# Reordering batch 0 between its ternary layer and its first softmax, in a float32 network of two attention and two feed-forward layers

## What is computed

```python
x = x + _L0_xattn_ref(_layernorm(x), fside_BxS2xS2_0, ctx_1024)     # int8-like quantised linear, silu, quantised linear
x = x + _L0_ffn_ref(_layernorm(x), w1, w2, w3)                      # ternary weights: sigmoid(x1) * x2, down
x = x + _L1_xattn_ref(_layernorm(x), ctx_1024, mask, Wq, Wk, Wv, Wo)  # 16 heads, softmax over 256 context rows
x = x + _L1_ffn_ref(_layernorm(x), router, sh_gate, sh_up, sh_down, r_gate, r_up, r_down)  # gated, plus routed part
```

## Time and profile before

| | us |
|---|---|
| median of 3 runs | 388.93 |
| lowest and highest | 388.9 and 389.31 |
| the profiled execution | 389.01 |
| its span, first to last instruction | 387.3 |
| TensorE busy in it | 377.5 (97%) |
| VectorE, ScalarE, GpSimd busy | 299.0, 233.2, 162.3 |

### The profile page before, as it was taken

How to read it: one execution, slowest core, us unless ns; L and a number is a source line. 1 busy time by engine, 2 the same in 40 slices (tenths; PEclk the granted TensorE clock), 3 DMA queues, 4 the chain that set the end, 5 groups by cost and what they waited for, 6 DMA issues and landing times.

```text
span 387.3 us, 8390 instructions
## 1 busy us (share of the span) xinstructions
PE 377.5 (97%) x2966; PEld 357.2 (92%) x2966; DVE 299.0 (77%) x982; ACT 233.2 (60%) x616; POOL 162.3 (42%) x260
## 2 busy tenths in 40 slices
PE   8899999999999999999999999999999999999996
PEld 7798789999899999999999999999999999999896
DVE  4798889889967889787767989787768876665644
ACT  1798787867544466766554466766554676664332
POOL 2113876874633344344443345246343333332232
PEclk9999999999999999999999999999999999999999
DMA  7999310000000200000000200000000000000000
GB/s 246 324 341 391 115 32 2 2 2 0 3 2 0 85 1 3 0 3 3 2 27 2 59 1 2 0 3 3 1 29 2 0 3 0 3 0 2 24 8 27
DMA packets 15193, 16.93 MB, mean 44 GB/s; under 512 B 1584, under 2 KB 14128, under 8 KB 15152
## 3 DMA queue, kind: packets, MB, share of 16 engines
q1 hardware_dynamic: 15152, 16.40, 13.0%
HBM read 15.34 MB, written 1.05 MB: 42 GB/s over the span
## 4 chain that ended last, share of the span: by engine, by line
PE 80%; DVE 11%; ACT 4%; POOL 2%; issue 2%; DVEq 0%; POOLq 0%
PE bank_qa L409 12%; PE bank_o L663 7%; PE bank_s L608 7%; PE bank_pt L628 7%; PE bank_u L644 7%; PE bank_s L409 5%; PE bank_o L667 4%; PE bank_s L616 3%; PE bank_u L648 3%; PE bank_s L526 3%; PE bank_pt L409 3%; PE bank_u L748 3%; PE bank_pt L556 2%; PE bank_pt L526 1%; PE bank_x L418 1%
## 5 line engine op out<-in xcount | busy, mean ns | idle before, releaser
L1318 POOL TENSOR_SCALAR prob<-prob,row_inv,valid_b 128x256 f32<-128x256 f32 x128 | 70.3, 559 | 84.9 <-DVE row_inv L1688 84.9
L1014 ACT ACTIVATE prob<-prob,row_min 128x256 f32<-128x256 f32 x128 | 64.2, 502 | 39.6 <-DVE row_min L1680 39.5
L1693 DVE TENSOR_TENSOR pt_lo<-bank_pt,pt_hi 128x512 fp32r<-128x512 f32 x64 | 43.9, 685 | 14.9 <-ACT pt_hi L967 14.9
L1680 DVE CUSTOM_DVE_ANT_0 prob<-bank_s,masked 128x256 f32<-128x256 f32 x128 | 48.5, 417 | 0.9 <-ACT masked L996 0.6
L1329 POOL TENSOR_TENSOR act_lo<-act_raw,act_hi 128x256 fp32r<-128x256 f32 x32 | 24.2, 755 | 44.3 <-ACT act_hi L1081 44.2
L967 ACT ACTIVATE pt_hi<-bank_pt 128x512 fp32r<-128x512 f32 x64 | 37.6, 587 | 4.0 <-PE bank_pt L628 3.8
L628 PE MATMUL bank_pt<-ident,prob 128*128 128x128 f32 x256 | 39.2, 274 | 0.4 <-POOL prob L1318 0.3
L608 PE MATMUL bank_s<-cxT_hi,qa_hi 128*128 128x256 f32 x128 | 37.9, 319 | 0.0
L409 PE MATMUL bank_qa<-xt_hi,a_hi 128*128 128x256 f32 x126 | 35.6, 283 | 0.0
L409 PE MATMUL bank_qa<-xt_lo,a_hi 128*128 128x256 f32 x126 | 35.5, 282 | 0.0
L409 PE MATMUL bank_qa<-xt_hi,a_lo 128*128 128x256 f32 x126 | 35.5, 282 | 0.0
(11 more groups left out here) (325 smaller groups left out, 1196.3 us busy)
## 6 DMA issues: line engine op xcount, KB each, us to landing
wq_raw<-in_wqT SPq DMA_DIRECT2D x4, 512.0 KB, 7.9
wo_raw<-in_wo SPq DMA_DIRECT2D x4, 512.0 KB, 8.4
w_raw<-in_w12T SPq DMA_DIRECT2D x2, 704.0 KB, 7.7
gate_raw<-in_gateT SPq DMA_DIRECT2D x2, 576.0 KB, 7.6
up_raw<-in_upT SPq DMA_DIRECT2D x2, 576.0 KB, 9.4
down_raw<-in_downT SPq DMA_DIRECT2D x2, 576.0 KB, 11.2
x<-in_x SPq DMA_DIRECT2D x4, 256.0 KB, 6.1
guT<-in_guT SPq DMA_DIRECT2D x4, 256.0 KB, 3.5
```

Of the source, the lines that this page charges most:

```text
L1014: act.activation(row, row, ACT.Exp, scale=-1.0, bias=row_min[:, h % 2, t:t + 1], accum_out=row_sum[:, h % 2, t:t + 1]).then_inc(S["s_exp"], 1)
L1318: pool.tensor_scalar(row, row, row_inv[:, h % 2, t:t + 1], valid_b[:, 0:1], ALU.mult, ALU.mult).then_inc(S["s_norm"], 1)
L1680: dve.tensor_tensor_reduce(out=prob[:, h % 2, t, :], in0=src[:, t * T:(t + 1) * T], in1=masked[:, :], scale=1.0, scalar=3.0e38, op0=ALU.ad ...
L1693: dve.tensor_tensor(pt_lo[:, :, cols], bank["pt"][:, :].rearrange("p (s t) -> p s t", s=2), f32(pt_hi[:, :, cols]), ALU.subtract).then_inc ...
```

## The change

Only the order of calls differs, on four engines. Nothing is added or taken away.

```diff
             scores(0, 1)
             queries(0, 2)
             queries(0, 3)
+            prep_unit(13)
             q_turn_xn(1)
-            prep_unit(13)
             prep_unit(14)
...
             prep_hi(10)
             prep_hi(11)
+            ln_hi(0, "lna", xt_hi)
             ffn_weights_hi(3)
-            ln_hi(0, "lna", xt_hi)
             prep_hi(12)
...
             exps(0, 0)
+            exps(0, 1)
             queries_hi(0, 1)
-            exps(0, 1)
             prep_hi(13)
...
             bit_low(0, 3)
+            bit_low(0, 4)
+            bit_low(0, 5)
             pool.wait_ge(S["ctx_hi"], 1)
             pool.tensor_tensor(cx_lo[:, :, :], cx[:, :, :], f32(cx_hi[:, :, :]), ALU.subtract)
             pool.tensor_tensor(cxT_lo[:, :], cxT[:, :], f32(cxT_hi[:, :]), ALU.subtract).then_inc(S["ctx_lo"], 1)
-            bit_low(0, 4)
-            bit_low(0, 5)
+            power(0, "lna")
             lnq_power(1, 2)
             ffn_weights_lo(0)
-            power(0, "lna")
             pool.wait_ge(S["lna_xn"], NT)
...
             bit_act(0, 4)
+            bit_act(0, 5)
+            q_weight_scales(1)
             dve.wait_ge(S["x1_stats"], 1)
             lnq_variances([1])
-            bit_act(0, 5)
-            q_weight_scales(1)
-            prep_lo(7)
             bit_residual(0)
             ln_stats_of(0, "lna")
+            prep_lo(7)
+            ln_apply(0, "lna")
             prep_lo(8)
-            lnq_apply(1)
-            ln_apply(0, "lna")
             prep_lo(9)
             prep_lo(10)
             ln_lo(0, "lna", xt_hi, xt_lo)
             prep_lo(11)
+            valid_batch(0)
+            lnq_apply(1)
             first_queries_lo(0)
             first_queries_lo(1)
-            valid_batch(0)
             row_minima(0, 0)
             row_minima(0, 1)
+            row_inverses(0, 0)
             prep_lo(12)
-            row_inverses(0, 0)
+            row_inverses(0, 1)
             queries_lo(0, 1)
-            row_inverses(0, 1)
             q_first_scales(1)
```

## The result

| | before | changed |
|---|---|---|
| median of 6 runs each, us | 388.91 | 390.98 |
| lowest to highest | 388.76 to 389.42 | 390.73 to 391.36 |
| span of the profiled execution | 387.3 | 389.2 |
| TensorE busy in it | 377.5 | 376.2 |

The ratio is 1.0052, with a 95% interval of 1.0041 to 1.0062: the change costs 2.07 us. The forecast was 390.0, with a range of 388.4 to 391.6.

The account below looks back on a forecast made before the run. TensorE, busy for 97% of the span, was taken as the bound. Profiled 389.01, +1.2 (part 4), -0.1 (part 5's gap shrinks) gave 390.1; the median, 0.08 lower, made it 390.0, range 388.4 to 391.6 us.

Parts of the forecast that it names:

- the gate at folding 10: Folding 10 writes bank qa, so must wait until prep_lo(7), now behind residual and statistics, has read it; start 44.27.
- the conflict at batch 1's norm: lnq_apply(1) on VectorE lands among GpSimd's big subtractions; its second half waits one out, 1.2 us lost.
- Part 1: Chunks 4 and 5 ahead of the context on GpSimd: TensorE's hole closes, gain up to folding 10 of 1.2 us.
- Part 2: Folding 7's low half behind residual and statistics: gives the gain back, folding 10 at 44.27, transposes 46.4 instead of 46.33.
- Part 3: ACT's xt_hi ahead of gate_hi: 0.18 us gained, first queries at 47.76 instead of 47.91.
- Part 4: valid_batch(0) and lnq_apply(1) ahead of the first queries' low halves: TensorE resumes at 51.43 instead of 50.20, 1.2 us lost.
- number 3: GpSimd's big weight subtraction ffn_weights_lo(3), counted from 0; expected to start at 49.3 to 49.5 and take about 1.41 us.
- rival 1: Both halves of batch 1's norm blocked if number 3 starts before 49.26: +2.6, 391.5 us; chance 0.17.
- Part 5: Head 1's exponentials ahead of queries_hi(0, 1), folding 13 ahead of q_turn_xn(1): at best 0.1 gained, at most 0.2 lost.
- Carrying to the end: From 58 us on orders are the old ones and TensorE nearly always busy, so a shift is carried to the end.
- Rival 3: Gap at 56.77 to 58.05 closes if batch 1's reduction starts by 53.9: TensorE gains 0.86, 388.1 us; chance 0.15.
- the prediction's sentence on the page: By the page's full two-port blocking, number 3 would start 0.35 later and the time would be 390.25.

Follow-up runs that it names:

- e6: Kernel before with part 1 alone: GpSimd makes the low halves of chunks 4 and 5 ahead of the context's; 388.41 us (ratio 0.9986).
- e5: Changed kernel with VectorE's order ahead of the residual as before: batch 1's variances before bit_act(0, 5), weight scales behind it; 390.52 us.
- e8: Kernel before with ACT's xt_hi alone moved ahead of the cast of gate_hi; 388.74 us (ratio 0.9994).
- e1: Changed kernel with one more wait: GpSimd starts weight subtraction number 3 only after VectorE has written batch 1's norm; 390.07 us.
- e2: Changed kernel with folding 7's low half back ahead of the residual; 392.14 us (ratio to before 1.0085).
- e7: Kernel before with part 5 alone: head 1's exponentials and inverses earlier, folding 13 ahead of batch 1's transposes; 389.10 us (ratio 1.0002).
- e4: Kernel before with valid_batch and batch 1's norm alone moved behind folding 11's low half, ahead of the queries' low halves; 390.10 us.
- e3: Changed kernel with folding 7's low half back ahead of the residual, batch 1's norm and power back ahead of batch 0's; 390.61 us.
- e9: Changed kernel with the edits of e5 and e3, and GpSimd's first weight subtraction behind batch 0's norm; 388.49 us (ratio to before 0.9984).

## Why the prediction was right, and where it was short

The direction held, and so did the two mechanisms, the gate at folding 10 and the conflict at batch 1's norm; the size, 1.1 us, is about half of the 2.07 measured. The 0.97 that is missing lies mainly ahead of the first queries, where the sum had a gain of 0.15 and the runs a loss of 0.63. Another 0.15 lies behind the low passes (0.05 later, where the sum had 0.1 sooner).

- **Part 1.** TensorE's hole went as foreseen. The gain to folding 10, put at 1.2 us, was too large: e6, the part alone, shows 0.73 (3.98 against 4.71). The four pairs of passes took 1.31 us and not four times 0.24, and folding 8 takes 1.00 and not 0.81, as the step from 42.41 to 43.41 in the earlier trace rows already had it. Folding 8's share had no weight in the sum, since the gate covers it; the slower passes also hold the residual, which waits for the last of them. The step that failed is the sentence that the weight scales and variances "are done by 41.0, so they cost nothing": they were done at 42.03, since L1514 and L1478 took 0.81 and 0.71 us. The group took 2.85, from 39.18 to 42.03, where I had 1.6. By e5 it cost 0.44, within the 0.5 that I had as its bound but had left out of the sum. Ahead of the change L1514 ran at the very end of a GpSimd operation, and its row did not show the risk. The residual started 2.73 us after folding 7, against 1.98 in my working.
- **Part 2.** The gate was there. From residual to the low half's start it took 2.01 us, exactly the term of the sum. It opened late because the residual was late: folding 10 lost 0.86 on before's place where I had 0. Of that, e5 gives 0.44 back; 0.31 is what the residual in e5 is still behind my working (2.29 against 1.98), mainly because of the slower passes of part 1; and the last 0.11 is that folding 10 starts 0.15 behind the end of the low half (44.75), where I had 0.04.
- **Part 3.** 0.23 us in e8, where I had 0.18 less a little.
- **Part 4.** The term was 1.2 us. Between first queries and low passes the changed kernel lost 1.39, to be compared with 1.2 and the 0.15 that I had gained up to there, 1.35 in all. e1 shows that 1.04 of it (12.66 to 11.62) is the conflict, the rest the mere place ahead of the low halves. Which half waited was the other way round: the first waited out number 3, since it was issued at 49.83, 0.1 behind that one's start, and the second went through while GpSimd was itself waiting for ACT. I had no such pause in my working. So number 3 had started ahead of the first half, which is the condition of rival 1. That one half waited and not both, as both did in e2, is in part luck, and with it that the term came out near its size.
- **Part 5.** Nothing gained, up to 0.2 lost: e7 shows 0.19 at the first mix; its runs cannot tell this from nothing.
- **Carrying to the end.** The shift at the first mix and that of the medians agree within 0.17 us for every kernel but e2 (2.40 and 3.16).
- **Rival 3** (faster) needed the reduction of batch 1 by 53.9. In the changed kernel it started at 56.31, and the second transposed head only at 59.26.
- **The two-port rule.** The Trainium skill (SBUF — State Buffer, section Who interferes with whom) says that, of a tensor_scalar in a two-port mode and a GpSimd instruction, the one issued later blocks fully. For the VectorE side the runs agree: in seven places a tensor_scalar ended 0.03 to 0.48 us behind a GpSimd subtraction (L1514, L1478 and L1487 of the changed kernel, L1487 of e2, e4 and e5, L1453 of e3). GpSimd was delayed less. Its up_lo subtraction started at 51.31, when L1487 had 0.30 us to run, and took 1.57 instead of 1.42. In e2, where a half had its turn between two of the four big subtractions, these took 5.59 us in all, against 5.58 in e9, where no norm ran beside them; so the last of them was not 0.35 late, as the prediction's sentence on the page has it.

## What to carry to other kernels

Moving an instruction in a hand-written order moves it beside other work on the other engines. Before a VectorE norm or scaling between SBUF tiles goes to a new place, look at what GpSimd does in that microsecond: on a path that TensorE waits for, one wait more on GpSimd (e1) was worth 0.9 us. And a gain in front is worth only what the next gate lets through: here one reader of a PSUM bank, a single low half behind the residual, made folding 10 start 1.61 us later (5.57 after folding 7 against 3.96 in e2).

## What the runs showed of the hardware that I had not expected

- The wait depends not on the size of VectorE's instruction but on GpSimd's: two numbers per partition (L1514, 0.19 us in the kernel before) took 0.81 us beside a pair of GpSimd subtractions, and batch 1's norm 0.73, 1.50, 1.78 or 2.38 us, by where in GpSimd's 1.39 us period it was issued.
- Reciprocals, reductions, aggregates and operations with one PSUM operand were not held in the same stretches (L1515 at 0.17 throughout, L1912 at 0.68), nor did GpSimd's small powers hold the norm (L1453 0.73 beside L1287 of the changed kernel); the power itself took 0.84 there instead of 0.70.
- A start that is 0.06 us too late is enough (e3): the subtraction started at 45.94, the norm at 46.00, and the norm paid 1.07 us.
